# One home for x2 with its id column, own slots for the second list's tiles, and byte addresses in a Post-LN layer with 14 experts

## The reference

```python
x = layernorm(x + attn(x))      # 16 heads of 8, causal softmax, projection, residual, an inner layernorm
logits = x @ gate_w.T           # 14 experts
top2_p, top2_i = top_k(softmax(logits), 2)
w = top2_p / top2_p.sum(-1)
hh = gelu(einsum('nd,edf->nef', x, w1) + b1)       # hidden size 256
out = einsum('nef,efd->ned', hh, w2) + b2
x = layernorm(x + clip(x + w0 * out[first] + w1 * out[second], -100, 100))
```

## Time and profile before

| what | value |
| --- | --- |
| median of three runs | 491.21 us (487.19 to 492.39) |
| span of the profiled execution | 485.0 us, 6.2 us under the median of the runs |
| PE, DVE, ACT, POOL busy | 364.4, 323.4, 263.2, 289.2 us |
| attention, mostly | 80 to 300 us |
| attention's end with the first list | 300 to 364 us |
| second list, first to last send | 369.34 to 447.90 us |
| results read back, weighted, stored | 450 to 485 us |

### The profile page before, as it was taken

How to read it: one execution, slowest core, us unless ns; L and a number is a source line. 1 busy time by engine, 2 the same in 40 slices (tenths; PEclk the granted TensorE clock), 3 DMA queues, 4 the chain that set the end, 5 groups by cost and what they waited for, 6 DMA issues and landing times. The chain is left out here.

```text
span 485.0 us, 12845 instructions
## 1 busy us (share of the span) xinstructions
PE 364.4 (75%) x4145; PEld 268.7 (55%) x4145; DVE 323.4 (67%) x1056; ACT 263.2 (54%) x624; POOL 289.2 (60%) x455
## 2 busy tenths in 40 slices
PE   4666998877897788889877686663968868778770
PEld 3434565555565455556544446563857757676570
DVE  7766587777886778677867746442636766662396
ACT  2026676676677667666755575432446445434054
POOL 7403365687768776876755447856555655566271
PEclk9679999899989999899988989877788897988995
DMA  5322334334333433342301312222422222220663
GB/s 138 99 71 70 89 93 124 94 92 131 98 98 96 129 97 95 101 124 79 107 24 57 59 46 57 77 55 73 131 73 81 61 67 73 71 80 3 201 212 108
DMA packets 72974, 44.02 MB, mean 91 GB/s; under 512 B 13233, under 2 KB 68931, under 8 KB 72796
## 3 DMA queue, kind: packets, MB, share of 16 engines
q1 hardware_dynamic: 66650, 33.11, 25.8%
q0 software_dynamic: 4640, 9.36, 6.0%
q10 hardware_dynamic: 1618, 0.73, 0.6%
HBM read 18.54 MB, written 12.36 MB: 64 GB/s over the span
## 5 line engine op out<-in xcount | busy, mean ns | idle before, releaser
L890 ACT ACTIVATE probs<-S 128x768 f32<-128x768 f32 x128 | 103.8, 811 | 59.9 <-PE S L1518 34.9
L757 POOL DMA_INDIRECT results<-tile_rows x77 | 76.8, 998 | 57.8 <-DVE tile_rows L1109 38.8
L1238 DVE TENSOR_REDUCE row_max<-S 128x4 f32<-128x1024 f32 x64 | 78.0, 1218 | 23.3 <-PE S L1553 20.2
L803 POOL DMA_INDIRECT sorted_rows<-x,row_no x64 | 65.6, 1025 | 35.9 <-DVE row_no L1270 22.0
L1572 PE MATMUL O<-probs,flat 128*32 128x256 f32 (+1 forms) x1024 | 58.8, 350 | 0.3 <-DVE row_chosen L1284 0.3
L1510 PE MATMUL S<-q_stack,k_stack 64*128 64x256 bf16 (+1 forms) x512 | 44.8, 254 | 16.6 <-ACT probs L890 14.0
L776 POOL TENSOR_SCALAR_AFFINE_SELECT probs<-probs 128x256 f32<-128x256 f32 x104 | 39.9, 407 | 23.5 <-ACT probs L890 23.2
L1238 DVE TENSOR_REDUCE row_max<-M 128x8 f32<-128x1024 f32 (+1 forms) x32 | 39.0, 1219 | 10.9 <-PE M L1553 10.9
L1572 PEld LDWEIGHTS O<-probs,flat 128*32 128x32 f32 x1024 | 27.8, 113 | 23.2 <-issue 7.4
L880 ACT ACTIVATE hT<-S,k_stack 128x128 f32<-128x128 f32 x76 | 24.8, 370 | 27.3 <-PE S L1618 14.0
L1547 PE MATMUL S<-k_stack,q_stack 64*128 64x256 bf16 (+1 forms) x320 | 27.4, 268 | 16.2 <-DVE row_max L1238 13.6
(11 more groups left out here) (271 smaller groups left out, 895.4 us busy)
## 6 DMA issues: line engine op xcount, KB each, us to landing
q_stack<-flat SPq DMA_DIRECT2D x96, 64.0 KB
k_stack<-flat SPq DMA_DIRECT2D x85, 64.0 KB
tile_rows<-sorted_rows SPq DMA_DIRECT2D x77, 64.5 KB
experts<-in_L_ffn_w_dram SPq DMA_DIRECT2D x28, 128.0 KB
xin<-in_L_attn_target_dram SPq DMA_DIRECT2D x16, 128.0 KB, 2.8
xres<-in_L_attn_target_dram SPq DMA_DIRECT2D x16, 128.0 KB
out_dram<-probs SPq DMA_DIRECT2D x8, 256.0 KB, 2.3
q_stack<-results SPq DMA_DIRECT2D x7, 256.0 KB, 3.2
```

Source lines behind the costliest of these rows:

```text
L757: pool.indirect_dma_start(results, bass.IndirectOffsetOnAxis(ap=y_rows[:, slot, D:ROW].bitcast(U32), axis=0), y_rows[:, slot, 0:D], None, ...
L803: pool.indirect_dma_start(sorted_rows, bass.IndirectOffsetOnAxis(ap=row_no[:, q * 2 * TT + n:q * 2 * TT + n + 1], axis=0), x2[:, q, n % 2, ...
L890: act.activation(probs[:, n].rearrange("p (a q) -> p a q", a=2), S[0][:, :].rearrange("p (a q) -> p a q", a=2)[:, :, 0:T + P], ACT.Exp, sc ...
L1238: dve.tensor_reduce(row_max[:, s % R, :, g0:g0 + ng, half], maxima_of[i][:, :].rearrange("p (a h k) -> p a h k", a=2, h=ng), X, ALU.max).t ...
```

## The change

Three things change together.

x2 lives in one tensor, `x2_all`, with 129 columns for every sequence. ACT writes it there once (now without a wait for the copies) and its two copies are gone. As each row now has one id column, the scatters go by choice: POOL writes the ids of choice 0, sends both blocks, waits until these two transfers have landed, writes the ids of choice 1, waits for that copy, and sends both blocks again. Readers of x2 read 128 of 129 columns.

The 47 tiles of the second list have a slot each, `late_rows`, in the storage of `probs`, which attention no longer needs then. SP loads them in 15 groups of 1 to 4 tiles; from the seventh group on a group waits until PE has turned the tiles of all groups up to six before it. POOL takes the ids from these slots, so DVE copies none in the second list; DVE's wait for an old send stands ahead of the y instead.

DVE no longer packs block numbers: one operation makes `rows_byte`, a table of byte addresses. SP loads two of them by one instruction and uses them as they are, with the rows as bytes, 516 to a row.

```diff
...
     LISTED = -(-K2 // XR) * XR
+    WORDS1, WORDS = K1 // XR, (K1 + LISTED) // XR
     assert K1 % XR == 0 and K1 <= LISTED <= P and (2 * G1 * T - E * (P - 1)) > (K1 - 1) * P
-    WORDS1, WORDS = K1 // XR, (K1 + LISTED) // XR
-    BLOCKS1, BLOCKS = K1 // 2, (K1 + LISTED) // 2
+    GROUPS = (1, 1, 2, 2, 3, 3) + (4,) * 8 + (3,)
+    assert sum(GROUPS) == K2
...
         rstd2 = sb("rstd2", [P, TT])
-        x2 = sb("x2", [P, R, 2, TT, ROW])
-        x2_all = sb("x2_all", [P, B, TT * D])
+        x2_all = sb("x2_all", [P, B, TT, ROW])
         x2T = sb("x2T", [P, R, T])
...
         late = probs[:, :, :].rearrange("p n q -> p (n q)")
+        late_rows = late[:, 0:K2 * ROW].rearrange("p (n c) -> p n c", c=ROW)
+        def rows_of(s):
+            return rows[:, s % XR] if s < K1 else late_rows[:, s - K1]
         OUT = 4
...
             sp.wait_ge(words_done, 2)
-            def blocks_of(i):
-                return sp.value_load(block_word[0:1, bass.ds(i, 1)], min_val=0, max_val=(1 << 2 * BLOCK_BITS) - 1)
-            first_blocks = {}
-            blocks = [0]
-            def load_rows(s, q, turn, is_tile):
-                if is_tile(s):
-                    if q % 2 == 0:
-                        blocks[0] = first_blocks[s // 2] if s // 2 in first_blocks else blocks_of(s // 2)
-                    n = (blocks[0] >> BLOCK_BITS * (q % 2)) & ((1 << BLOCK_BITS) - 1)
-                    n = n.with_bounds(min_val=0, max_val=E * (REGION // P))
-                    wait_apart(sp, rows_turned, s - XR + 1, ids_copied)
-                    sp.dma_start(rows[:, q], sorted_rows[bass.ds(n * P, P)]).then_inc(rows_in[q], 16)
-            for w in range(XR // 2):
-                first_blocks[w] = blocks_of(w)
+            blocks = E * (REGION // P) * BLOCK_BYTES
+            at_pair = []
+            def bytes_of(s):
+                if not at_pair:
+                    at_pair.extend(nc.values_load_multi_w_load_instructions(
+                        rows_byte[0:1, s:min(s + 2, K1 if s < K1 else TILES)], engines=[mybir.EngineType.SP], min_val=0, max_val=blocks,
+                        skip_runtime_bounds_check_because="the table is made with a min against the highest block")[1])
+                return at_pair.pop(0)
+            row_bytes = sorted_rows.rearrange("n c -> (n c)").bitcast(U8)
+            def load_rows(s, at):
+                n = row_bytes[bass.ds(at, BLOCK_BYTES)].rearrange("(p c) -> p c", p=P)
+                return sp.dma_start(rows_of(s).bitcast(U8), n)
             for i in range(R):
...
             for s in range(K1):
-                early_tile(load_rows)(s)
+                at = bytes_of(s)
+                after(sp, rows_turned, s - XR + 1)
+                after(sp, ids_copied, s - XR + 1)
+                load_rows(s, at).then_inc(rows_in[s % XR], 16)
             sp.wait_ge(iotas, 6)
...
             sp.wait_ge(words_done, 4)
-            for w in range(BLOCKS1, BLOCKS1 + XR // 2):
-                first_blocks[w] = blocks_of(w)
             for i in range(R):
...
             sp.wait_ge(pieces_sent, 16)
-            run_tiles(sp, load_rows)
+            sp.wait_ge(pv_done, 4 * B)
+            for g, tiles_in in enumerate(GROUPS):
+                if g >= XR:
+                    sp.wait_ge(rows_turned, K1 + sum(GROUPS[:g - XR + 1]))
+                for n in range(sum(GROUPS[:g]), sum(GROUPS[:g]) + tiles_in):
+                    load_rows(K1 + n, bytes_of(K1 + n)).then_inc(rows_in[g % XR], 16)
             for q in range(YR):
...
                     pool.wait_ge(y_biased, s - 4)
-                    pool.indirect_dma_start(results, bass.IndirectOffsetOnAxis(ap=y_rows[:, slot, D:ROW].bitcast(U32), axis=0),
+                    ids = y_rows[:, slot, D:ROW] if s - 5 < K1 else rows_of(s - 5)[:, D:ROW]
+                    pool.indirect_dma_start(results, bass.IndirectOffsetOnAxis(ap=ids.bitcast(U32), axis=0),
                                             y_rows[:, slot, 0:D], None, bounds_check=2 * N - 1, oob_is_err=False).then_inc(sent[slot], 16)
...
                             pool.wait_ge(iotas, 4)
-                        after(pool, scattered[(r - 6) % R], 16 * 2 * TT * ((t - 6) // R))
-                        pool.tensor_copy(x2[:, (r - 6) % R, :, :, D].bitcast(U32),
-                                         place[:, t - 6].rearrange("p i k -> p k i")).then_inc(placed, 1)
+                        pool.tensor_copy(x2_all[:, t - 6, :, D].bitcast(U32), place[:, t - 6, :, 0]).then_inc(placed, 1)
                     if u == 0 and on(t - 5):
...
                         if n == 0:
-                            pool.wait_ge(placed, t - 5)
-                            pool.wait_ge(x2_twice, t - 5)
+                            pool.wait_ge(placed, 2 * (t - 6) + 1)
+                            pool.wait_ge(x2_done, t - 5)
                             pool.wait_ge(row_ready, t - 5)
-                        pool.indirect_dma_start(sorted_rows, bass.IndirectOffsetOnAxis(
-                            ap=row_no[:, q * 2 * TT + n:q * 2 * TT + n + 1], axis=0), x2[:, q, n % 2, n // 2], None).then_inc(scattered[q], 16)
+                        k, i = n // TT, n % TT
+                        if n == TT:
+                            pool.wait_ge(scattered[q], 16 * 2 * TT * ((t - 6) // R) + 16 * TT)
+                            pool.tensor_copy(x2_all[:, t - 6, :, D].bitcast(U32), place[:, t - 6, :, 1]).then_inc(placed, 1)
+                            pool.wait_ge(placed, 2 * (t - 6) + 2)
+                        at = q * 2 * TT + 2 * i + k
+                        pool.indirect_dma_start(sorted_rows, bass.IndirectOffsetOnAxis(ap=row_no[:, at:at + 1], axis=0),
+                                                x2_all[:, t - 6, i], None).then_inc(scattered[q], 16)
                     if u == (0 if early(t) else 3) and on(t):
...
                         after(act, scattered[(r - 5) % R], 16 * 2 * TT * ((t - 5) // R))
-                        after(act, x2_kept, t - 5)
                         for i in range(TT):
-                            last = act.activation(x2[:, (r - 5) % R, 0, i, 0:D], ys[:, i], ACT.Identity, bias=centre2[:, i:i + 1],
+                            last = act.activation(x2_all[:, t - 5, i, 0:D], ys[:, i], ACT.Identity, bias=centre2[:, i:i + 1],
                                                   scale=rstd2[:, i:i + 1])
...
                             act.dma_start(q_stack[SHIFT:P:TILE, 0], shift_t[0:H * TT, 0]).then_inc(shifted, 16)
-                    if u == 7 and on(t - 5):
-                        act.wait_ge(x2_done, t - 4)
-                        act.copy(x2[:, (r - 5) % R, 1, :, 0:D], x2[:, (r - 5) % R, 0, :, 0:D]).then_inc(x2_twice, 1)
                     if u == 7 and on(t - 2):
...
                         act.mul(shift_t[H * TT:2 * H * TT, (r - 2) % R], M[1][H * TT:2 * H * TT, 0:P], -1.0).then_inc(shift_copied, 1)
-                    if u == 7 and on(t - 5):
-                        act.copy(x2_all[:, t - 5].rearrange("p (i d) -> p i d", i=TT), x2[:, (r - 5) % R, 0, :, 0:D]).then_inc(x2_kept, 1)
                     if u == 7 and on(t - 3):
...
                     dve.tensor_copy(expert_now[q], experts[:, bass.ds(e * SIZE, SIZE)]).then_inc(expert_ready, 1)
-                if is_tile(s - 1):
+                if is_tile(s - 1) and s - 1 < K1:
                     after(dve, sent[(s - 1) % YR], 16 * ((s - 1) // YR))
...
                 if is_tile(s - 5):
+                    if s - 5 >= K1:
+                        dve.wait_ge(sent[(s - 5) % YR], 16 * ((s - 5) // YR))
                     dve.wait_ge(layer2_done, s - 4)
...
                 dve.tensor_tensor(tile_at[:, :], tile_no[:, :], done[:, 0:1], ALU.add).then_inc(first_table, 1)
-            def pack(of, n, word0, block0, lists):
-                ne, nb = n // XR, n // 2
+            def pack(of, first, n, word0, lists):
+                ne = -(-n // XR)
                 dve.wait_ge(tile_turned, lists)
-                dve.tensor_tensor(expert_part[:, 0:n].rearrange("p (i q) -> p i q", q=XR),
-                                  of[0:1, 0:n].rearrange("p (i q) -> p i q", q=XR),
+                dve.tensor_scalar(rows_byte[:, first:first + n], of[0:1, P:P + n], float(E * (REGION // P)), float(BLOCK_BYTES),
+                                  ALU.min, ALU.mult).then_inc(words_done, 1)
+                dve.tensor_tensor(expert_part[:, 0:ne * XR].rearrange("p (i q) -> p i q", q=XR),
+                                  of[0:1, 0:ne * XR].rearrange("p (i q) -> p i q", q=XR),
                                   expert_unit[:, None, :].broadcast_to([1, ne, XR]), ALU.mult).then_inc(tile_parts, 1)
-                dve.scalar_tensor_tensor(out=block_part[:, 0:n].rearrange("p (i q) -> p i q", q=2),
-                                         in0=of[0:1, P:P + n].rearrange("p (i q) -> p i q", q=2), scalar=float(E * (REGION // P)),
-                                         in1=block_unit[:, None, :].broadcast_to([1, nb, 2]),
```

(10 more changed lines are left out.)

54 lines of the change are left out of this document (30 added, 24 removed).

## The result

The changed kernel takes 493.76 us (median of six runs, 491.76 to 496.25) against 491.8 us of the kernel before (six runs, 484.51 to 493.45). The ratio is **1.0106, 95% interval 1.0058 to 1.0154**: about 5 us slower. Ratios compare fast runs alone, those within 1.5% of the fastest of their kernel, while medians take in all runs, so the two can differ. Forecast were 480.4 us and a range of 468 to 493. Both sign and size were wrong. The profiled execution has a span of 494.2 us and is the slowest of its six runs, 496.25 us; so its 9.2 us over the span before show more than the runs do.

What follows compares the result with a forecast made beforehand. PE was taken to bound attention; in the second list no engine was full, with gaps between groups of sends. -6.5 - 3.3 - 1.0 = -10.8 us from the 485.0 span gave 474.2, plus 6.2 kept: 480.4 us, range 468 to 493.

Steps and rivals of the forecast that it cites:

- POOL's scatters: Attention: new landing wait, id copy and its wait before the third scatter, taken up by POOL's later idle time: 0.
- The second rival: Attention: scatters land late, POOL stands in its new wait and delays the selects; slower, case put at 500 us, chance 0.17.
- SP's loads: Second list: fewer SP instructions shorten the steps between sends, 6.5 us for the last 23 tiles, 3.3 for the first 23.
- The first rival: Lists: the slow motion is the sends' own, SP only its second victim; no gain there, 489.7 us, chance 0.30.
- ACT's copies: Attention: removing ACT's two x2 copies, 12.7 us of ACT, gains 0 because PE's row hides them; bound 12.7.
- DVE's id copies: Second list: removing 47 copies, 6.6 us of DVE, gains 0 because they lie beside the sends; bound 6.6.
- The base: Whole kernel: the runs' median stands 6.2 us above the profiled span of 485.0 us, and this difference is kept.
- DVE's weight copies: Expert's weights: copy takes 0.50 us alone, 0.72 beside a send; read as DVE waiting, against the skill page's opposite reading.

Runs made afterwards that it cites:

- x2 part alone: Kernel before with only the new single home of x2 (no ACT copies, ids written twice by POOL, landing wait): ratio 1.0104, 494.6 us.
- the change without the step: Changed kernel with x2 in two homes again, one ACT copy, both ids written ahead, no wait between scatters: ratio 0.9978, 488.9 us.
- the change with two pauses: Changed kernel with two small POOL copies, read by nobody, behind each send of the second list: ratio 1.0011, 491.8 us.
- the list part: Kernel before with only own slots, no id copies in the second list and byte addresses; x2 as before: ratio 0.9965, 488.1 us.
- the byte addresses alone: Kernel before with only SP's short loads by byte address; shared slots, DVE's id copies and x2 as before: ratio 0.9987, 487.9 us.
- the run with dead copies: Changed kernel with two x2 copies put back on ACT at the old places, into storage nothing reads: ratio 0.9993, 493.0 us.

## Why the prediction was wrong, point by point

- **POOL's scatters, priced at 0: the step that failed for the sign.** It saw that 0.19 + 0.30 us of POOL's time remain, and said that "POOL's next idle time, 1.86 us at 206.87, takes them". That idle time lies behind the third scatter, three pairs of selects and the fourth scatter, and all that stands ahead of it on POOL is later by the 0.26 us. The runs showed a cost in place of the 0: 1.04% for the x2 part alone, 1.23% for two small copies at that place in the kernel before, and none (0.9978) for the change without the step. The bound for this term was put at the landing, and not at the copy that the same sentence counted. By which way the step costs time is not shown, and about half of the 5 us goes with a lower clock.
- **The second rival had the place and not the mechanism.** It asked for a landing above 3.7 us. In the steady part of attention the landing was past when POOL came, 3.9 us behind the second scatter. Only in the thirteenth sequence, where POOL comes sooner, did it set the time in some profiles, by 0.64 us in the change with two pauses. The rule of the Trainium skill ("DMA: Bandwidth & Descriptors", Latency and other measured facts), a longer answer of HBM under load, did not decide: whatever it added in the steady part, the landing took less than 3.9 us. (The 2.56 us that it took for the last four sequences is the step of the last alone; the other three have 2.77 to 3.50.)
- **SP's loads, priced at -9.8 us: the step that failed for the size.** The 6.5 us for a silent SP rested on eight sends behind SP's last load, "the only stretch of that kind". The last seven steps of the changed kernel, with SP as silent, take 10.84 us and not 9.97, so these seven steps are no measure of SP's part. In the changed kernel SP is silent for 46 us, and the 23 last steps of y take 36.2 us against 35.8 before. The term was worth about 1.7 us: that much the list part gave (0.35%), and so much less is y with the short loads. The first rival, that SP is the second victim, was right in this part.
- **ACT's copies and DVE's id copies, priced at 0.** No run shows a gain from either: the change has no ACT copies and lost, and the byte addresses alone did as well as with the id copies gone. Whether ACT's missing copies cost something, the run with dead copies leaves open.
- **The sum.** Where -10.8 us were forecast, the list part gave -1.7 and the x2 part +5.1, each with an interval of about ±2.3 us.
- **The base.** The forecast kept 6.2 us between span and median. In the later runs the profiled execution's time is about 2 us over its span (496.25 and 494.2), so the span of 485.0 belongs to a run near 487, the fastest of the three shown: some 2 us of the 6.2 lie outside the span, and the rest is that run's distance from the median. This moved no sign.
- The rule weighed with DVE's weight copies (the Trainium skill, "SBUF — State Buffer", SBUF: two separate sides, the "DVE blocks DMA" trap) would have made the copies the cause of the gaps. With pauses between the sends the gaps went, and the copies were all there, so the copies alone do not make them.

What stays open: how the sends hold up PE and SP, and at which pace this begins; by which way the step on POOL costs time; and how it meets TensorE's clock. Sequences that run partly at the lower level took 17.4 to 17.9 us in the change and 16.4 to 17.2 before, and the change's profile has more of them (6 of 10 sequences, 4 before). Whether the step brings the lower clock about, no run shows.

## What to carry to other kernels

When a step on an engine is called hidden, look at all that stands between it and the idle time which is to take it up: the idle time only helps what stands behind it. Where the trace shows nobody who waits, that is no proof either: a small copy, put alone at the place and once more at another, told what the trace did not. A short stretch at the end of a loop, where the other engines run out of work, is no measure of what the loop would do without one part. And a queue that sends as fast as it can may hold up others: spacing its sends by a few tenths of a microsecond was worth more (0.9978 to 0.9871) than the list part with its shorter loads (1 to 0.9965).

## What the runs showed of the hardware

While POOL's indirect sends of 128 rows followed each other 1.27 us from start to start, SP's move before a load took 0.71 us where it takes 0.03, and gaps of 2 us came between groups of sends. With two small copies behind each send (1.61 us from start to start on average) there was no such gap, and with one (1.34 us at the least) there were three. Blocks of the same size written by SP's plain transfers, one to two a tile at 1.27 us a tile, left SP's move at 0.03 us. A copy on POOL takes 0.18 us, and a transfer that needs it starts 0.29 us behind it, where it idles 0.17 us behind another operation anyway: with the copy ahead of it, the third scatter came 0.25 us later.
